# A graph-attention kernel: the score maximum moved into the edge block, exponentials by head, division in pieces, and growing lags in the last stage

## The reference, cut to what matters

```python
feats = relu(x @ w1 + b1) @ w2 + b2                       # per head, 64 columns
x_cat = concatenate([feats[row], feats[col], elem[:, None]])
e1 = leaky_relu(relu(x_cat @ a1 + ab1) @ a2 + ab2, 0.2)   # one score per edge and head
w = exp(e1 - max(e1))                                     # one maximum per head over all edges
pooled = segment_sum(w[:, None] * feats[col], row)
row_sum = segment_sum(w, row) + 1e-10
out = layernorm(x + pooled / row_sum)
```

## Time and profile before

| | |
|---|---|
| device time, median of 3 | 3283.1 us (3279.12 to 3284.18) |
| profiled execution, first to last instruction | 3281.0 us |
| PE busy | 92%, 66% in weight loads |
| DVE busy | 81% |
| ACT busy | 56% |
| POOL busy | 54% |
| HBM traffic | 201 GB/s over the span |

### The profile page before, as it was taken

How to read it: one execution, slowest core, us unless ns; L and a number is a source line. 1 busy time by engine, 2 the same in 40 slices (tenths; PEclk the granted TensorE clock), 3 DMA queues, 4 the chain that set the end, 5 groups by cost and what they waited for, 6 DMA issues and landing times. The chain is left out here.

```text
span 3281.0 us, 58096 instructions
## 1 busy us (share of the span) xinstructions
PE 3017.2 (92%) x15765; PEld 2162.7 (66%) x15765; DVE 2643.2 (81%) x8931; ACT 1851.5 (56%) x4206; POOL 1769.3 (54%) x1691
## 2 busy tenths in 40 slices
PE   5888999799999949999999999999999999995774
PEld 3555666466666637777777777777777777772442
DVE  7998998655555548888888888888888888878995
ACT  3444555355555525566655655656655655654885
POOL 2776677577777635444444444444444444402776
PEclk9999999899999969999999999999999999997997
DMA  5888997456565645555545545555555555525984
GB/s 164 271 269 283 330 314 232 158 192 210 191 209 191 206 138 168 192 167 178 190 166 181 185 169 184 180 168 189 176 169 192 173 172 192 169 99 175 284 280 147
DMA packets 343600, 648.29 MB, mean 198 GB/s; under 512 B 43230, under 2 KB 250762, under 8 KB 343462
## 3 DMA queue, kind: packets, MB, share of 16 engines
q1 hardware_dynamic: 261174, 411.39, 37.6%
q0 software_dynamic: 75744, 232.45, 21.9%
q10 hardware_dynamic: 6544, 2.89, 0.4%
HBM read 338.64 MB, written 322.05 MB: 201 GB/s over the span
## 5 line engine op out<-in xcount | busy, mean ns | idle before, releaser
L1182 POOL TENSOR_TENSOR u_hc<-u_hc 128x1536 f32<-128x1536 f32 x98 | 270.1, 2756 | 724.8 <-DVE u_h L1342 687.9
L994 PE MATMUL bank<-w_node,xT 128*128 128x384 f32 x1564 | 567.4, 491 | 26.0 <-ACT bank L612 26.0
L1454 PE MATMUL bank<-xh,w1h 128*128 128x512 f32 x1568 | 528.3, 418 | 18.2 <-DVE xl L1371 14.5
L1257 ACT ACTIVATE hidT<-bank,b1c 128x512 f32<-128x512 f32 x392 | 269.7, 688 | 455.4 <-PE bank L1454 383.3
L1454 PE MATMUL bank<-xh,w1l 128*128 128x512 f32 x1568 | 494.2, 396 | 0.0
L1454 PE MATMUL bank<-xl,w1h 128*128 128x512 f32 x1568 | 494.1, 396 | 0.0
L1365 DVE TENSOR_SCALAR hidT<-bank,b1c 128x512 f32<-128x512 f32 x392 | 294.3, 751 | 170.7 <-PE bank L1454 167.4
L612 ACT ACTIVATE bank<-bias_all 128x512 f32<-128x512 f32 x391 | 234.2, 599 | 330.6 <-DVE H L705 330.2
L994 PEld LDWEIGHTS bank<-w_node,xT 128*128 128x128 f32 x1564 | 281.3, 192 | 176.2 <-ACT bank L612 29.1
L1469 PE MATMUL bank<-hidT,w2f 128*64 128x256 f32 x3136 | 360.1, 382 | 0.9 <-issue 0.9
L1380 DVE STREAM_TRANSPOSE feat<-catT 32x256 f32<-32x256 f32 x784 | 342.8, 437 | 17.8 <-ACT catT L1266 2.9
(11 more groups left out here) (279 smaller groups left out, 6110.9 us busy)
## 6 DMA issues: line engine op xcount, KB each, us to landing
hc_tab<-H SPq DMA_DIRECT2D x78, 960.0 KB
er<-edge_tab SPq DMA_DIRECT2D x98, 512.0 KB, 4.4
X<-in_x SPq DMA_DIRECT2D x78, 640.0 KB, 5.1
h_row<-hc_tab SPq DMA_DIRECT2D x97, 512.0 KB, 7.5
out_x<-o_row SPq DMA_DIRECT2D x97, 512.0 KB, 2.9
hc_tab<-zero_row SPq DMA_DIRECT2D x10, 4032.0 KB
hc_tab<-zero_row SPq DMA_DIRECT2D x9, 3840.0 KB
edge_tab<-u_x SPq DMA_DIRECT2D x98, 256.0 KB, 5.6
```

What stands on the lines that cost most here:

```text
L994: ins = t_.matmul(p[:, 0:384], xT[t // 2 % XR][:, t % 2, c * P:(c + 1) * P], w_node[:, c, :], start=False, stop=c == 1, skip_group_check=True)
L1182: g.tensor_tensor(c, c, u_hc[s][:, :, MULT:MULT + 3].unsqueeze(3).to_broadcast([P, 4, 3, P]), ALU.mult).then_inc(u_scaled, 1)
L1257: a.activation(hidT[m][:, :], bank[2 + m % 2][:, :], ACT.Relu, bias=b1c[:, m:m + 1])\
L1454: ins = t_.matmul(bank[2 + m % 2][:, :], w[:, c, m * P:(m + 1) * P], xx[s][:, c, :], start=n == 0, stop=n == 5)
```

## The change

**In the edge block.** The score step adds `ab2` while it moves the scores (so L1650 goes). At step 100 DVE takes, before the last pair's `feat_0`, the leaky relu, the padding and the maximum over the first 194 columns (`most_so_far`), turns both halves of the last pair's features at once, and after the last `dots` does the same for the last two columns (`most_of_all`). The maximum over partitions is no longer POOL's: PE turns `mx` from 128x4 to 4x128, DVE reduces it to one value per head, PE turns that back to all partitions, DVE negates it (`mx_less`). A one-element exponential at the end of ACT's queue makes the table load fall in this block.

**At the start of the last stage.** ACT takes four exponentials, one per head, with `mx_less` as bias, and then a one-element root. DVE no longer prepares `raw`. The division runs in seven pieces (`WEIGHTS`, columns 0, 12, 24, 40, 64, 96, 140, 196): the first before the loop's first pair, the others in iterations 5, 11, 19, 31, 47 and 69. `w_end` and the two small values move to iterations 50, 56 and 62.

**In the loop.** `staged` replaces `straight`: the lag of a stage depends on the pair. Statistics run at lag 1 for pairs 0 to 5, 2 up to pair 19 and 3 from there; scale and shift at 1, 3 and 4; norm at 1, 3 and 5. `seed` and `choose` run one pair ahead for the first six. `variance` is gone: ACT's root takes epsilon as its bias. The order of the stages on DVE is another.

```diff
+                def most(lo, hi, k):
+                    dve.wait_ge(sc_done, hi // 2)
+                    part_ = score[:, lo:hi, :]
+                    st.done(v.scalar_tensor_tensor(out=part_, in0=part_, scalar=0.2, in1=part_, op0=ALU.mult,
+                                                   op1=ALU.max))
...
+                def most_of_all():
+                    most(ET - 2, ET, 1)
+                    st.wait()
+                    v.tensor_tensor(mx[:, 0, :], mx[:, 0, :], mx[:, 1, :], ALU.max).then_inc(mx_ready, 1)
+                    dve.wait_ge(mx_turned, 1)
+                    v.tensor_reduce(mx_row[0:HEADS, :], bank[0][0:HEADS, 0:P], AX.X, ALU.max).then_inc(mx_found, 1)
+                    dve.wait_ge(mx_spread, 1)
+                    st.done(v.tensor_scalar(mx_less[:, :], bank[1][:, 0:HEADS], -1.0, None, ALU.mult))
...
+        def stat_lag(t):
+            return 1 if t < 6 else 2 if t < 20 else 3
+
+        def scale_lag(t):
+            return 1 if t < 6 else 3 if t < 20 else 4
...
+        def staged(n, ring, stages):
+            for k in range(-1, n + 5):
+                for fn, lag in stages:
+                    for t in range(max(0, k - 5), min(n, k + 2)):
+                        if t + lag(t) == k:
+                            fn(t, t % ring)
...
-                pool.wait_ge(mx_ready, 1)
-                g.partition_all_reduce(mxa[:, :], mx[:, :], P, bass.bass_isa.ReduceOp.max).then_inc(mxa_ready, 1)
...
-                a.activation(wgt[:, :, :], raw[:, :, :], ACT.Exp).then_inc(w_ready, 1)
+                for h in range(HEADS):
+                    a.activation(wgt[:, :, h], score[:, :, h], ACT.Exp, bias=mx_less[:, h:h + 1]).then_inc(w_ready, 1)
+                a.activation(table_try[:, :], zero_row[:, 0:1], ACT.Sqrt)
...
-                straight(ET // 2, RING, [(root, 3), (seed, 0), (choose, 0), (norm, 5)])
+                staged(ET // 2, RING, [(root, stat_lag), (seed, ahead), (choose, ahead), (norm, norm_lag)])
...
+                def divide(u, s):
+                    for lo, hi in zip(WEIGHTS, WEIGHTS[1:]):
+                        if 2 * u == max(lo - 2, 0):
+                            run = back[:, ET - hi:ET - lo, :]
+                            st.done(v.tensor_scalar(run, run, 1e-10, None, ALU.add))
+                            st.wait()
+                            st.done(v.reciprocal(run, run))
+                            st.wait()
+                            v.tensor_tensor(wgt[:, lo:hi, :], wgt[:, lo:hi, :], run[:, ::-1, :], ALU.mult)\
+                                .then_inc(den_ready, 1)
...
                 def weigh(u, s):
+                    dve.wait_ge(den_ready, len([lo for lo in WEIGHTS[:-1] if lo <= 2 * u]))
...
-                straight(ET // 2, RING, [(stat, 3), (weigh, 0), (aggr, 3), (scale, 4), (add, 0), (finish, 0), (variance, 3),
-                                         (shift, 4)])
+                staged(ET // 2, RING, [(divide, at_once), (weigh, at_once), (stat, stat_lag), (aggr, stat_lag),
+                                       (add, at_once), (finish, at_once), (scale, scale_lag), (head_totals, at_once),
+                                       (shift, scale_lag)])
```

More of the change, by code:

```diff
@@ L1415, in relu_7, with last, most_so_far @@
                     relu(u, 7)
+                def last(u):
+                    return isinstance(u, int) and u == US - 1
                 def feat_0(u, s):
                     turn_feat(u, s, 0)
+                    if last(u):
+                        turn_feat(u, s, 1)
                 def feat_1(u, s):
-                    turn_feat(u, s, 1)
+                    if not last(u):
+                        turn_feat(u, s, 1)
+                def most(lo, hi, k):
[4 more added lines that the diff above has]
+                    st.wait()
+                    st.done(v.tensor_tensor(part_, part_, pad_neg[:, lo:hi].unsqueeze(2)
+                                            .to_broadcast([P, hi - lo, HEADS]), ALU.add))
+                    st.wait()
+                    st.done(v.tensor_reduce(mx[:, k, :], part_.rearrange("p t h -> p h t"), AX.X, ALU.max))
+                def most_so_far(u, s):
+                    if last(u):
+                        most(0, ET - 2, 0)
+                def most_of_all():
[6 more added lines that the diff above has]
+                    st.done(v.tensor_scalar(mx_less[:, :], bank[1][:, 0:HEADS], -1.0, None, ALU.mult))
+                    st.wait()
                 def dots_0(u, s):
@@ L1542, in build @@
         z_st, z_mv = tmp("z_st", [P, 2 * RING, 6]), tmp("z_mv", [P, 2 * RING, 2])
-        z_v, z_d, z_r, z_b = (tmp(n, [P, 2 * RING]) for n in ("z_v", "z_d", "z_r", "z_b"))
+        z_d, z_r, z_b = (tmp(n, [P, 2 * RING]) for n in ("z_d", "z_r", "z_b"))
         fix_e, fix_z, fix_o = tmp("fix_e", [P, 2 * D]), tmp("fix_z", [P, D]), tmp("fix_o", [P, D])
@@ L1621, in root @@
                 def root(u, s):
-                    act.wait_ge(zvar, u + 1)
-                    a.activation(z_d[:, 2 * s:2 * s + 2], z_v[:, 2 * s:2 * s + 2], ACT.Sqrt).then_inc(zsd, 1)
+                    act.wait_ge(zmv, 2 * u + 2)
+                    if u == 0:
+                        act.wait_ge(at_ready, 1)
+                    a.activation(z_d[:, 2 * s:2 * s + 2], z_mv[:, 2 * s:2 * s + 2, 1], ACT.Sqrt, bias=eps_c[:, 0:1])\
+                        .then_inc(zsd, 1)
                 def norm(u, s):
@@ L1648, in _ @@
                 st.done(v.tensor_scalar(fix_row[:, :], head_n[:, 0:1], 1.0, 1.0, ALU.max, ALU.subtract))
-                for h in range(HEADS):
-                    st.done(v.tensor_scalar(score[:, :, h], score[:, :, h], ab2b[:, h:h + 1], None, ALU.add))
+                st.done(v.memset(eps_c[:, :], EPS))
                 st.wait()
@@ L1673, in _ @@
                                         stops_back[:, :].unsqueeze(2).to_broadcast([P, ET, HEADS]), ALU.mult))
[L1674 to L1675 removed]
+                st.done(v.memset(agg[RING - 1][:, 1, :], 0.0))
                 st.wait()
@@ L1678, in _ @@
                     st.done(v.tensor_tensor_scan(back[:, :, h], goes_back[:, :], back[:, :, h], 0.0, ALU.mult, ALU.add))
-                st.done(v.tensor_reduce(fix_w[:, 0, :], w_end[:, :, :], AX.X, ALU.add))
-                st.done(v.memset(agg[RING - 1][:, 1, :], 0.0))
                 st.wait()
-                st.done(v.tensor_scalar(back[:, :, :], back[:, :, :], 1e-10, None, ALU.add))
-                st.done(v.tensor_scalar(fix_w[:, 1, :], w_sum[:, ET - 1, :], 1e-10, None, ALU.add))
-                st.done(v.tensor_scalar(fix_w[:, 2, :], fix_w[:, 0, :], 1e-10, None, ALU.add))
```

80 lines of the change are left out of this document (46 added, 34 removed).

## The result

The changed kernel takes 3317.2 us (median of 4, 3315.9 to 3318.9) against 3283.6 us of the kernel before (median of 4, 3279.1 to 3286.2): 1.0103 times as long, 95% interval 1.0091 to 1.0115, or 33.6 us more. The forecast was 3298 us. The direction was right, the size was not, and the time lies outside the range.

What follows compares the result with a forecast made beforehand. The prediction took PE to bound the edge block and POOL to end the kernel, with DVE becoming the loop's bound. -2.0 - 19.3 + 53.9 - 17.9 = +14.7 us gave 3298 us, range 3277 to 3308 (8 in 10).

Steps and rivals of the forecast that it cites:

- The bound passes from POOL to DVE: Last stage's loop: DVE's iteration at 3.00 us exceeds POOL's 2.68 a pair, so DVE sets the pace.
- z_st to z_mv 0.90, z_r to z_b 0.20: DVE's loop: start-to-start times of operations right behind their input, instead of 0.67 and 0.05 to 0.07 us.
- The head: Last stage's start to first `weigh`: 7.2 us instead of 26.5, so -19.3 us (-17 to -20).
- PE keeps its clock: Loop: against the rival that PE falls to half clock for good, about +97 us, 3395 us, chance 0.03.
- the first rival: Loop: waits between dependent operations are free, 2.44 us an iteration, POOL stays the bound; 3262 us, chance 0.12.
- The tail, 12.6 us: Last `weigh` to fix put: 12.6 us (11 to 14) instead of 30.5, no POOL backlog; -17.9 us.
- its signs of being wrong: DVE at 2.7 us or less between starts, POOL's puts without gaps, last put about 20 us after last `weigh`.
- The loop, 3.00 us an iteration: First to last `weigh`: 3.00 us an iteration (2.83 to 3.06) against 2.51; +53.9 us (+38 to +60).
- The two terms where the sequencer can't run ahead: DVE's loop: agg behind z_mv taken at 0.18 us, `weigh` behind z_b at 0.22 us.
- The edge block, nothing: Edge block's loop: a sum instead of a copy over 8 elements on DVE costs nothing, since PE is busy throughout.
- The seam, -2.0: Edge block's end to last stage: last stage starts at 2964.4 instead of 2966.4, -2.0 us (-2.7 to 0).

Runs made afterwards that it cites:

- e1: Changed kernel with only DVE's loop order edited (stat ahead of weigh, scale ahead of add): 3280.0 us, 0.9986 times the kernel before.
- e2: Kernel before with only DVE's loop order changed to the new one, at the old fixed lags: 3334.9 us.
- f3: Changed kernel in its own order, with lags that stop growing at 2, 3 and 3: 3317.0 us.
- e4: Changed kernel without the separate signal on DVE between the wait for z_st and aggr: 3305.6 us.
- h1: Kernel before with one unused tensor of 56 bytes a partition ahead of wgt: 3287.6 us.
- f2: Changed kernel with e1's order and fixed lags 2 (statistics), 3 (scale, shift) and 3 (norm): 3266.2 us, 0.9949 times the kernel before.
- f4: Changed kernel with scale moved ahead of add on DVE, all else in the new order: 3299.9 us.

## Why the prediction was off

Right, by its own steps:

- *The bound passes from POOL to DVE.* It decided the sign. e1 turns it back with the order alone, e2 brings it about with the order alone.
- *z_st to z_mv 0.90, z_r to z_b 0.20*: 0.90 and 0.20. Both had been read where the old loop runs out.
- *The head*: 26.5 to 7.2 us, from rows of a trace that had none of the new operations; the first `weigh` at 2976.6 instead of 2971.6 only because the stage began later. That it fits to the tenth is luck: what stands ahead of the sums took 0.9 instead of 1.1, the first piece of the division 1.1 instead of 0.95, and one exponential by head took 0.57 instead of 0.35, which the masks still covered.
- *PE keeps its clock*: 2.4 GHz from 3020 us to the last `weigh`, with 1.12 us of idle ahead of most `join`s. It fell once before that, around 3015 after 2.01 us of idle (that `join` took 1.54 us instead of 1.10), and came back; idle times of 2.22 us ahead of the `join` at 3039.67 and of 3.17 ahead of that at 3200.03 did not bring it down. So the length of one pause, which the prediction held against this rival, does not tell when the clock falls.

The Trainium skill's rule that a chain of Vector operations costs the same with a semaphore behind each ("VectorE: DVE Perf Modes", section "The DRAIN you can't avoid") would have made the first rival the outcome, 3262 us. e1 and e2 measure what it leaves out: the same operations take 0.64 us (e1) and 0.63 us (e2) more per iteration in the order in which they wait for their neighbour. (The advice on the number of operations stands in the same page's "Rules for kernel authors".) By its text the rule compares chains with a signal behind each operation; of a next operation that waits for the signal it says nothing, and that is what costs here.

Wrong, by size. Two steps failed above all: the tail, where the prediction put POOL's backlog at nothing, and the loop, where it took too little for the places at which DVE's sequencer can't run ahead.

- *The tail, 12.6 us: measured 20.0.* This is the largest single error, 7.4 us. The step added DVE's four last iterations and the correction and said that POOL had no backlog. It has none while DVE sets the pace, but with norm at lag 5 seven pairs are unput at the last `weigh`; DVE then finishes them in 1.3 us each and POOL needs 2.58. f3 shows it by shortening the lag. A fix put about 20 us behind the last `weigh` stood in the prediction among its signs of being wrong, for a POOL that is the bound; it came true although DVE was the bound.
- *The loop, 3.00 us an iteration: measured 3.08.* The two terms where the sequencer can't run ahead were taken at 0.18 and 0.22 out of 0.16 to 0.22 and 0.07 to 0.25, and agg to the next at 0.90. They are 0.24, 0.21 and 0.92. The bound for agg's four waits came from a row where z_r alone stood ahead of them, without the separate signal that stands ahead of z_mv; without that signal it is 0.18 here too (e4). The prediction's own bounds add to 3.07, where it wrote 3.06, and 3.08 is above either. The 86 iterations of the full pattern at 0.08 are 6.9 us. The rest nearly cancels: seven iterations have an extra pause of 0.36 us that was not in the sum and that no experiment explains, 2.5 us, and the divisions, the border operations and the first iterations took some 2.6 us less than assumed.
- *The edge block, nothing: measured +4.0.* What the change does to DVE there costs nothing. What it does to the places of the tensors wasn't thought of; h1 shows two thirds of the longer step, the rest is open, and 0.5 us are scatter of the start.
- *The seam, -2.0: measured -1.0.* The last `scores` took 2.06 us behind 4.94 us in which PE stood idle, and the dots with it 5.9 us (2960.83 to 2966.77) instead of 5.3; and from the negation's end at 2968.82 to the first instruction of the last stage are 0.57 us, where 0.2 were assumed. The two turns on PE took 1.3 us from the end of the last maximum (2967.55) to the end of the negation, not far from the assumed 1.5.

The range was too narrow for a sum of five terms, four of which erred to the same side: its high end held 3.08 us an iteration and a tail of 14, and no error in the edge block or at the seam.

## What to carry to other kernels

Look at who reads whom between neighbours in a queue before looking at what each operation costs: on DVE an operation right behind its input started 0.04 to 0.15 us after the input's end, one that reads something older 0.08 us before the end, and in a loop of 2.5 us this was the difference between being under and over the next engine's pace. An engine that sets no pace in the loop may still set the end: count what it has in flight at the last input, times its own period. And starting an output stream earlier is worth nothing unless the stream is the bound from then on without pauses; with e1's order, constant short lags beat growing ones here (f2 against e1).

## What the runs showed of the hardware that was not expected

- A wait or signal that the sequencer handles by itself is free as long as the operation ahead of it is long, and costs 0.06 to 0.11 us each behind a short or late one: without the signal behind `z_st` an iteration is 0.17 us shorter (3.08 to 2.91), of which 0.11 at its own place and 0.06 ahead of agg; the two sequencer entries ahead of `weigh` cost 0.14 together behind z_r and z_b and nothing behind agg (f4).
- 56 unused bytes a partition ahead of the edge block's tensors lengthened its loop by 2.7 us of 1704 in one execution (17.643 to 17.667 us a step in steps 60 to 85), with no instruction changed; the added time lies in PE's products of the hidden layer.
- POOL's indirect DMAs of 128 rows were never issued faster than one in 1.29 us in any of the fifteen traces; the profile counts 0.98 of that as busy. Occasional longer ones make it 1.34 in the mean in the kernel before, where POOL, busy for 39 of 50 us, is at its limit.
